# Two fused attention and feed-forward layers: one loop over token groups becomes, per layer, an unrolled attention phase and an unrolled feed-forward phase

## The reference, cut to what matters

```python
x = x + xattn0(layernorm(x), ctx)     # x: 32 batches x 56 tokens x 256; ctx: 32 x 1500 x 64
x = x + moe(layernorm(x))             # 16 experts, top 4 of 2 groups of 4, and a shared expert; inner width 128
x = x + xattn1(layernorm(x), ctx)
x = x + lora_ffn(layernorm(x))        # hidden width 704; 8 LoRA experts of rank 16, top 2

def xattn(h, kv_c, ...):              # 16 heads
    q_r    = rope(h @ Wq.T @ w_kc_q) @ W_qr     # layer 1 has no rope on the queries
    kv_r   = rope(kv_c)
    scores = q_r @ (kv_r @ W_kr).T              # 16 x 56 queries against 1500 keys
    ctx_c  = softmax(scores) @ kv_r
    return (ctx_c @ w_kc_kv.T) @ Wo.T
```

## Time and profile before

| | |
|---|---|
| median of 3 runs | 3398.19 us (3393.26 to 3401.04) |
| profiled execution, whole | 3397.9 us |
| its span, first to last instruction | 3396.1 us |
| mean granted TensorE clock | 0.919 |
| PE, DVE, POOL, ACT busy share of the span | 87%, 59%, 52%, 37% |
| score stages, each of 4 groups | about 232 us in layer 0, 212 us in layer 1 |

### The profile page before, as it was taken

One profiled execution on the slowest core, in us unless ns is written; L12 is line 12 of the kernel. 1 busy time (PEld: TensorE's weight loads), 2 busy tenths in 40 slices (PEclk: granted clock), 3 DMA queues, 4 the chain that ended last, 5 costly groups with the idle time before them and its releaser, 6 DMA issues. The chain is left out here.

```text
span 3396.1 us, 43529 instructions
## 1 busy us (share of the span) xinstructions
PE 2958.6 (87%) x16008; PEld 1691.4 (50%) x16008; DVE 2015.0 (59%) x2351; ACT 1262.0 (37%) x1747; POOL 1759.2 (52%) x1008
## 2 busy tenths in 40 slices
PE   7689978899888998879998699878998799779988
PEld 6444456444465444754446444354445344454435
DVE  3576556766567674676655566455655565455645
ACT  3134434244341443423443334323442244323432
POOL 0467724677336774366763167504761277216750
PEclk9789989899988999898998799998998799888999
DMA  7423213233123331142321423104311332132310
GB/s 256 120 62 91 59 41 95 74 82 82 35 80 88 75 84 47 61 112 58 84 56 50 111 60 78 57 10 98 79 35 49 87 74 57 52 74 60 79 57 6
DMA packets 117806, 247.54 MB, mean 73 GB/s; under 512 B 30415, under 2 KB 82879, under 8 KB 110038
## 3 DMA queue, kind: packets, MB, share of 16 engines
q1 hardware_dynamic: 117590, 244.57, 27.1%
HBM read 171.24 MB, written 48.27 MB: 65 GB/s over the span
## 5 line engine op out<-in xcount | busy, mean ns | idle before, releaser
L1218 POOL TENSOR_TENSOR sums<-sums,prob 125x896 f32<-125x896 f32 x528 | 1117.9, 2117 | 141.8 <-ACT prob L1105 88.5
L1334 DVE TENSOR_REDUCE maxpart<-pair 112x2 f32<-112x1000 f32 x720 | 861.5, 1197 | 444.2 <-PE pair L854 444.1
L1105 ACT ACTIVATE prob<-wide 125x896 f32<-125x896 f32 x768 | 704.6, 917 | 882.8 <-PE wide L880 882.8
L895 PE MATMUL single<-prob,kv 125*64 125x448 f32 x3072 | 756.0, 571 | 0.9
L875 PE MATMUL wide<-qhigh,kparts 64*125 64x448 f32 x3072 | 461.9, 379 | 0.0
L854 PE MATMUL pair<-kparts,qhigh 64*112 64x500 f32 x1440 | 356.9, 491 | 61.7 <-DVE maxpart L1334 48.4
L854 PEld LDWEIGHTS pair<-kparts,qhigh 64*112 64x112 f32 x1440 | 129.1, 175 | 489.2 <-DVE maxpart L1334 398.4
L1218 POOL TENSOR_TENSOR sums<-prob 125x896 f32<-125x896 f32 x64 | 134.9, 2108 | 411.7 <-ACT prob L1105 411.7
L875 PEld LDWEIGHTS wide<-qhigh,kparts 64*125 64x125 f32 x3072 | 283.4, 187 | 110.0 <-issue 81.2
L880 PE MATMUL wide<-shift,ones_row 64*125 64x448 f32 x1536 | 289.8, 372 | 46.4 <-DMA shift<-maxrow 46.4
L875 PE MATMUL wide<-qlow,kparts 64*125 64x448 f32 x1536 | 288.2, 370 | 0.0
(11 more groups left out here) (322 smaller groups left out, 4235.4 us busy)
## 6 DMA issues: line engine op xcount, KB each, us to landing
kparts<-keys_merged SPq DMA_DIRECT2D x64, 750.0 KB, 9.1
wexp_low_values<-in_experts SPq DMA_DIRECT2D x68, 384.0 KB, 3.1
kparts<-kparts SPq DMA_DIRECT2D x96, 250.0 KB, 3.1
keys_merged<-kparts SPq DMA_DIRECT2D x32, 750.0 KB, 7.6
recip<-zrec_merged SPq DMA_DIRECT2D x112, 112.0 KB, 2.8
raw<-in_ctx SPq DMA_DIRECT2D x33, 375.0 KB
w_low_values<-w_merged SPq DMA_DIRECT2D x64, 192.0 KB, 3.3
values_merged<-kv SPq DMA_DIRECT2D x32, 375.0 KB
```

What stands on the lines that cost most here:

```text
L895: mm = pe.matmul(mix_acc[64 * half:64 * half + DC, 0:HQ], kv[:, j % 3, t, :], prob[:, (j * LT + t) % NPROB, half * HQ:(half + 1) * HQ], st ...
L1105: nc.scalar.activation(prob[:, n_ % NPROB, :].rearrange("p (a b) -> p a b", a=2), acc[0:LP, :, 0:HQ], ACT.Exp)\
L1218: nc.gpsimd.tensor_tensor(dst, first_in, prob[:, n_ % NPROB, :], ALU.add).then_inc(s["pool_sum"], 1)
L1334: V.tensor_reduce(maxpart[:, j % 2, t:NMAX:4, b], acc[0:TQ, :, 0:LB], AX.X, ALU.max).then_inc(*R.signal_drained(kind, *key))
```

## The change

The hardware loop is gone. `attention`, `experts` and `lora_ffn` replace `run_layer`: a layer does the attention of all 32 batches in one block, then the feed-forward of all four groups in one block, each unrolled, with one barrier at the end. The tokens of all groups stay on chip in `x_all`, loaded once at the start; `x_mid` and the block ahead of the loop are gone. `POOL_LAST`, the tiles of a group's last batch that POOL sums, goes from 5 to 7. Expert and LoRA weights are loaded and split once, and sit on chip for all groups. Matmuls, sums and maxima of a group are the same in number.

```diff
-POOL_TILES, POOL_LAST = 11, 5
+POOL_TILES, POOL_LAST = 11, 7
...
+def attention_schedule(layer):
...
+    for g in range(G):
+        first, old = BG * g, BG * g - 1
+        if layer == 0:
+            for n in range(H + 1):
+                if n + SPLIT_AHEAD < H:
+                    add("wsplit", g, n + SPLIT_AHEAD)
+                if n < H:
+                    add("qwide", g, n, region=n % 2)
+                if g and n == 0:
+                    add("mix", old, LT - 1)
+                    add("context", old)
+                if g and n == 1:
+                    add("norm", old, region=3)
...
+                if g and n == 5:
+                    add("spread", old)
+                if g and n == 8:
+                    add("share", old, 2)
...
+            if g:
+                add("attn", g - 1, 0, region=1)
...
+                if g + 1 < G and j == BG - 1:
+                    if t == 2:
+                        add("mean", g + 1, region=3)
+                    if t in (3, 4):
+                        add("square", g + 1, t - 3)
+                    if t == 5:
+                        add("var", g + 1, region=3)
+                    if t in (7, 8):
+                        add("rstd", g + 1, t - 7)
+                    if t == 9:
+                        add("xsplit", g + 1)
...
+def moe_schedule():
...
+    for u in range(G * (E0 + 1)):
+        g, i = divmod(u, E0 + 1)
...
+        add("gateup", u, region=u % 2)
...
+        add("hidden", u)
+        if u:
+            add("down", u - 1)
+        if u and i == 0:
+            add("out", g - 1)
+        if g + 1 < G and i and i - 1 < 7 + RANKS:
+            ahead(g + 1, i - 1)
...
+def ffn_schedule():
...
+        add("gateup", u, 0, region=0)
+        if more and m == 0:
+            add("mean", g + 1)
...
+        if more and m == 5:
+            add("lora", g + 1)
+        if u:
+            add("down", u - 1)
+        add("gateup", u, 1, region=1)
+        if u and m == 0:
+            add("loradown", g - 1)
+            add("out", g - 1)
...
-    with nc.Fori(0, G) as g:
```

2480 lines of the change are left out of this document (1394 added, 1086 removed).

## The result

The changed kernel takes 3258.24 us (median of 4 runs, 3250.99 to 3261.43) against 3399.61 us measured beside it: ratio 0.958, interval 0.9554 to 0.9606. The forecast was 3123, with a range of 3040 to 3205. It is faster, as forecast, but by 141 us, not by 275.

What follows compares the result with a forecast made beforehand. PE was taken as full in the score stages and elsewhere waiting in serial chains at low clock. Terms -80, -70, -5, -60, -49, -11 sum to -275, from the 3396.1 us span to 3121; forecast 3123, range 3040 to 3205.

Steps and rivals of the forecast that it cites:

- The experts: Layer 0 expert phase: weights loaded once, next group's norm and routing among the experts; 346 us instead of 416, -70.
- The layer 0 score stage: Layer 0 join: takes over `mean`, `var`, key transposes and waits, less a warm clock at its start; +6.5 us.
- six key transposes 3.7: Term of the layer 0 score stage: PE's transposes for the keys moved into it, 3.7 us.
- The layer 0 query stage: Layer 0 join: projection and last `mix` come in, idle time fills, keys move out; 78.4 becomes 76, -2.4 us.
- The 13.2 us for the fill of the last maxima: End of layer 0's query stage: projection pieces fill 8.2 us idle and give back 5 by the clock.
- the 5 us for the keys moved out: Layer 0 query stage: moving out the second batch's keys frees about 5 us of PE transposes and a rotation wait.
- The LoRA phase: Layer 1 feed-forward: weights loaded once, next group's norm and routing among the blocks; 307 us instead of 356, -49.
- the routing head of 20.0 us runs partly behind it: LoRA entry: routing runs partly behind 27 us of weight loading and splitting; 34 us until blocks run freely.
- A: Rival: norm and rank pieces that wait on DVE and ACT hold up experts or exponentials; 3252 us, chance 0.14.
- B: Rival: the 60 us of waits charged to joins, experts and LoRA part are not there; 3063 us, chance 0.18.
- D: Rival: the change does not do what it says, an unseen wait chains the groups; 3400 us, chance 0.01.
- C: Rival: slower, the clock stays low outside the score stages, in experts, blocks and query stages; 3585 us, chance 0.04.

Runs made afterwards that it cites:

- raw_late: Changed kernel with each raw context load issued at the batch's last tile, behind the shift, not ahead of the reciprocals' store: 3209.82 us.
- rot_late: `combo` with GpSimd's layer 0 rotation of the next context moved from a batch's last tile to its first: 3139.54 us.
- attn_last: Changed kernel with all four projection quarters in layer 0 behind the last maximum: 3268.52 us.
- attn_early: Changed kernel with layer 0's first projection quarter right behind the last head's product, the others one per two maxima: 3244.34 us.
- keys_kept: `combo`, but the keys of a group's second batch stay in the last batch of the group before: 3158.42 us against 3160.54.
- loraz_first: Changed kernel with VectorE making `lora_z` behind the last `down`, ahead of the second half of the next block: 3234.12 us.
- ctx_half: `combo` with `ctx_n` made in two halves, one behind each of a batch's last two maxima: 3149.51 us.
- combo: Changed kernel with later raw loads, second-batch keys in the query stage, earlier projection, alternating layer 1 maxima, early `lora_z`, earlier LoRA `down` and `rank`: 3160.54 us.

## Why the prediction was wrong, point by point

**Right in kind, and in size in part by luck.** The experts: 340.8 us, forecast 346. Their groups follow at 75.5 us where 76 to 80 was named and 78 charged, at full clock, and in much of a group an expert comes every 3.84 us. Group 0 took 100.6 us where 92 was charged:

```profile
1484.50:1585.10 100.60, 76.42 (x348) 65.24 (x349) 68.15 (x113) 37.19 (x59) 28.41 (x15) 0.90 0.05 19
1585.10:1660.60 75.50, 71.95 (x355) 63.87 (x355) 52.01 (x95) 26.23 (x42) 0.00 (x0) 1.00 0.00 1
```

TensorE stands 14.2 us there for the routing (`moe_cw`), and the first expert weight comes 24.0 us into the stage, where it came after 20.2 in the kernel before, though only two experts stand ahead of it and not three. Entry and group 0 were 10 us too low, the three groups behind them with the end 15 too high, and the sum came out 5 us off. Two rows of the mean that belongs to the group after (start, length), and two steps of one kind in successive experts:

```profile
1596.42 1.67 PE L1247 MATMUL single<-x_all,mean_w 128*128 128x448 f32 x4
...
1711.12 0.37 PE L1285 MATMUL single<-moe_cwT,pick 112*128 112x448 f32 x1
1714.96 0.37 PE L1285 MATMUL pair<-moe_cwT,pick 112*128 112x448 f32 x1
```

The first has its like at 1671.92. The way into layer 1 (18.8 against 19) and layer 1's joins (query 48 against 46, score 214.9 against 213.5) came out within 2 us. The turnarounds and tails went as said. The next group's first `qwide` starts 3.0 us after the last shift product in layer 0, where within 1 us was named, and 0.8 in layer 1; about 2 of the 3.0 are idle.

**The layer 0 score stage, +6.5 forecast, +13.6 measured (21 of the 128 us).** The step that failed is "six key transposes 3.7". It counted the instructions that PE issues for a batch's keys and not what SyncE issues with them, the raw context load for two batches later. In the kernel before no load went with the last three batches. That load delays the reciprocals' store and the shift behind it. The kernel before showed the whole price: a middle batch with keys and a load 30.8 us, batch 6 without either 25.7. The price of a moved step was to be read as a difference between two batches, not as a sum of products. As an estimate from the table of batches, that gives 5.1 for each of batches 6 and 7 and 2.0 for batch 5, which had keys without a load (30.8 against 28.8), 12.2 us in place of 3.7; the stage missed by 7.1. Of the 5.1 us, 1.6 are transposes. `raw_late` took 0.9 off a middle batch (29.9) and `rot_late` 1.4 more (28.5), the wait for the load and the meeting with GpSimd that came in its place; the remaining 1.2 are not taken apart. (The terms written down for this stage add up to 6.2, not 6.5.)

**The layer 0 query stage, -2.4 forecast, +10 measured (38 us).** Two terms were too good. The 13.2 us for the fill of the last maxima: `attn_last` shows 3.0 for the order as it is, `attn_early` 7.3 for a better one. I took "the projection's four pieces stand just there" for a fill of all 8.2 us, but the idle pieces and the half clock lay ahead of the first piece. And the 5 us for the keys moved out were there, as `keys_kept` shows, but a new wait ate most of them in the changed kernel: `norm` of the group before, 1.4 to 1.7 us late in the three joins, in one of them 1.74 us with 5.7 us at half clock behind it (heads' products 1.12 us apart in place of 0.62), because of the same late reciprocals. No row was looked at for when `ctx_n` and the last sums would be ready there.

**The LoRA phase, 307 forecast, 369.0 measured (62 us).** The waits in a group are 13.3 us against 10, so the kind was right; on top come 6.1 against 3 for `loradown`, and half clock behind other waits. That makes 12 us for each of groups 1 and 2 (84.8 against 73). The entry took 44 us to the first block, 10 more than forecast: I had taken the loading of weights for its limit, and TensorE waits for the selection chain, 13.6 us ahead of `mask`, and 4.5 us more for `tok` ahead of the first block. The 27 us for loading and splitting came out: the last split ends 26.8 us into the phase, 1.0 us before `mask` begins. The step that failed is "the routing head of 20.0 us runs partly behind it": 17 us came behind the last split, where 7 were charged. What a shorter chain would give there was not measured. Group 0 took 76 us in place of 69. Group 3 was given 56 + 2 and took 79.3: from the last `down` of group 2 to its own first it is 17.4 us in place of 7.9, for the `loradown` of the group before (11.3 in `loraz_first`), and the end of the program was hardly in the sum; from its last `down` on the kernel before took 16.3 us, the changed one 17.3.

**Up to the first `qwide`, +7.** VectorE has the first context's rotation ahead of the norm's squares, and its tables are loaded in this phase now and no longer at the start:

```profile
120.14 1.82 DVE L1051 TENSOR_TENSOR rope_c<-raw,cosk 125x384 f32<-125x384 f32 x2 [8.96 <-DMA sink<-in_sink]
```

The prediction counted loads and barriers there and not this wait.

**The rivals.** A, "the chains show through", gave 3252, 6 us from the measured time, and had 0.14. It is right for the LoRA phase alone, in part: there the interleaving returned 8.4 us a group, by one execution. In the experts it returned 18, and the 58 us of layer 0 have another cause. So A's number came out by luck. B and D fell. C, half clock outside the score stages, also fell: 0.95 in the experts, 0.86 in the LoRA phase, 0.92 in the query stages; but the forecast of 0.96 or more for the mean was missed at 0.943, and I had let no term stand for the clock in the LoRA phase.

**The rule that was weighed.** I had left the shared port out of the sum, on the ground that the last batch has no maxima on VectorE. In the last batch that holds: two squares took 3.07 us together, 1.8 more than two of 0.62, and the products 0.62 each, so leaving out the 8 us was right. In middle batches the port cost the changed kernel nothing that shows, `ctx_n` took 0.62 us there; it cost some 1.3 us a batch once the loads were out of the way, and so has no share in the prediction's miss that these runs show. The Trainium skill's rule (SBUF — State Buffer, Who interferes with whom) fits what was measured then; `rot_late` and `ctx_half` are its test: 0.62 against 2.31 us, and half the data no faster.

**What stays open.** Why the granted clock stayed at 0.88 in one of three groups in which TensorE issued small products while it waited, and rose in the other two, is not settled. Nor was tried what `mean` in the LoRA phase's second region costs; in `combo` TensorE still stands 2.4 us there in each group.

## What to carry to other kernels

When a step moves, price it by a stretch that has it against one that has not; the difference holds its DMAs, its place in the queues and the waits of others, and a sum of its own instructions doesn't. A small transfer whose landing someone waits for must not be sent right behind a large one; reordering the small ones only hands the wait from one engine to the next. If the waits of an unrolled phase are each 2 to 4 us, look for the next wait in the queue of the engine that is named, ahead of the late instruction.
